# Choosing experts for the last eight attention pairs one step later, and reordering the scatters around it

## What is computed

```python
x = x + _L0_xattn_ref(_layernorm(x), ctx, ctx, mask, Wq, bq, Wk, bk, Wv, bv, Wo, bo)
# FFN on xt = x of the line above, per token:
router_logits = xt @ Wr + br
gates = max(softmax(router_logits)); idx = argmax(router_logits)
xn = layernorm(xt) * ln_g + ln_b
h = relu(xn @ W1[idx] + b1[idx]);  y = (h @ W2[idx] + b2[idx]) * gates
out = xt + y
```

## Time and profile before

| what | value |
|---|---|
| median of 3 runs (lowest to highest) | 268.44 us (268.17 to 268.88) |
| the profiled execution's own time, and its span | 265.34 us, 263.5 us |
| busy: PE, DVE, ACT, POOL | 243.8, 218.1, 171.7, 141.7 us |
| indirect DMA issues on POOL to DRAM (line 430) | 32, mean 1017 ns |
| last softmax shift begins (line 836) | 157.05 us |
| first expert matmul (line 1208) | 180.45 us |
| last expert matmul ends | about 254.5 us |

### The profile page before, as it was taken

The page is one execution under the profiler, slowest core; times in us unless marked ns, Lnnn a source line. Parts: engine busy times, 40 slices in busy tenths (PEclk is TensorE's granted clock), DMA queues, the critical chain, the costliest instruction groups (busy, mean ns, idle before and its releaser), DMA issues.

```text
span 263.5 us, 9102 instructions
## 1 busy us (share of the span) xinstructions
PE 243.8 (93%) x3204; PEld 191.2 (73%) x3204; DVE 218.1 (83%) x690; ACT 171.7 (65%) x339; POOL 141.7 (54%) x170
## 2 busy tenths in 40 slices
PE   8799999999999999999996999897999999999960
PEld 3266676785876777776854768446999999999950
DVE  7776878998999989987989897765889999999950
ACT  2697886876875967868754345004588888888820
POOL 3764363356658667765766546740454545454550
PEclk9999999999999999999999999999999999999996
DMA  7779980000000000000000100034122131222100
GB/s 190 236 226 348 412 348 6 2 2 7 20 13 13 13 24 21 16 10 23 13 23 21 36 23 23 31 115 107 50 55 72 50 87 57 74 72 65 42 23 0
DMA packets 17483, 19.55 MB, mean 74 GB/s; under 512 B 2703, under 2 KB 13332, under 8 KB 17440
## 3 DMA queue, kind: packets, MB, share of 16 engines
q1 hardware_dynamic: 14016, 14.15, 17.0%
q0 software_dynamic: 2272, 4.27, 4.7%
q10 hardware_dynamic: 1152, 0.57, 0.9%
HBM read 14.11 MB, written 5.33 MB: 74 GB/s over the span
## 4 chain that ended last, share of the span: by engine, by line
PE 69%; DVE 17%; issue 5%; POOL 3%; DMA 2%; POOLq 1%; ACT 1%; DVEq 0%; SPq 0%; ACTq 0%
PE ps L1208 13%; PE ps L1219 13%; PE ps L1026 8%; PE ps L1039 8%; PE ps L1132 7%; DVE Pr L836 5%; DVE mx L829 4%; PE ps L1065 4%; PE ps L1128 4%; PE ps L1011 3%; PE ps L1096 3%; PE ps L1201 2%; PE ps L1066 1%; PE ps L1103 1%; PE ps L1052 1%
## 5 line engine op out<-in xcount | busy, mean ns | idle before, releaser
L526 POOL DMA_INDIRECT out<-ot,G x39 | 37.8, 970 | 44.4 <-DVE ot L995 44.1
L551 ACT ACTIVATE PT<-ps 128x512 f32<-128x512 f32 x64 | 34.7, 594 | 31.8 <-PE ps L1039 31.6
L829 DVE TENSOR_REDUCE mx<-ps 128x16 f32<-128x1024 f32 x32 | 39.2, 1224 | 11.7 <-PE ps L1132 11.1
L430 POOL DMA_INDIRECT rows_dram<-row,posi x32 | 32.5, 1017 | 17.2 <-issue 9.6
L469 POOL TENSOR_TENSOR Kb<-KT,hmask 128x512 f32<-128x512 f32 x32 | 33.2, 1039 | 15.8 <-PE ps L1132 13.7
L1026 PEld LDWEIGHTS ps<-VB,PT 128*64 128x64 f32 x1024 | 32.4, 138 | 12.1 <-issue 12.1
L598 ACT ACTIVATE Pr<-Pr,rowany 128x1024 f32<-128x1024 f32 x32 | 36.8, 1149 | 4.3 <-DVE Pr L836 4.2
L836 DVE TENSOR_TENSOR Pr<-ps,mx 128x1024 f32<-128x1024 f32 x32 | 38.9, 1214 | 0.2
L1026 PE MATMUL ps<-VB,PT 128*64 128x18 f32 x1024 | 35.5, 212 | 0.0
L1039 PE MATMUL ps<-ident,Pr 128*128 128x128 f32 x256 | 34.7, 278 | 0.0
L1208 PE MATMUL ps<-xg,WR 128*128 128x128 f32 x248 | 32.8, 275 | 0.0
(11 more groups left out here) (133 smaller groups left out, 420.0 us busy)
## 6 DMA issues: line engine op xcount, KB each, us to landing
WA<-in_wpk SPq DMA_DIRECT2D x8, 578.0 KB, 11.0
G<-rows_dram SPq DMA_DIRECT2D x39, 66.0 KB, 1.9
X<-in_x SPq DMA_DIRECT2D x8, 256.0 KB, 6.1
C<-in_ctxT SPq DMA_DIRECT2D x8, 256.0 KB, 6.3
XT<-in_xT SPq DMA_DIRECT2D x8, 256.0 KB, 6.7
out<-ot,G POOLq DMA_INDIRECT x39, 2.2
rows_dram<-row,posi POOLq DMA_INDIRECT x32, 2.3
rows_dram<-empty ACTq DMA_DIRECT2D x6, 66.0 KB, 1.9
```

What stands on the lines that cost most here:

```text
L430: g.indirect_dma_start(out=rows, out_offset=bass.IndirectOffsetOnAxis(ap=posi[:, r, k:k + 1], axis=0), in_=row[:, r, k, E:E + RW], in_offs ...
L526: g.indirect_dma_start(out=out, out_offset=bass.IndirectOffsetOnAxis(ap=G[:, q, D + 1:D + 2].bitcast(I32), axis=0), in_=ot[:, q, :], in_of ...
L551: a.activation(PT[:, p % 2, 512 * m:512 * m + 512], ps[:, 4 + m, :], ACT.Copy).then_inc(freed[4 + m], 1)
L829: v.tensor_reduce(out=mx[:, i % 2, :], in_=psS.rearrange("p g (i k) -> p g i k", k=S), axis=AX.X, op=ALU.max).then_inc(s_mx, 1)
```

## The change

Five edits belong together:

- Unit 5 is scaled, picked and turned into one-hot rows in step 28 and ranked in step 29 (before: 27 and 28). Its ranks now share bank 7 with unit 6's second projection; its row numbers, gate and totals follow in step 30.
- Unit 6 is picked and made one-hot in step 31, after the softmax shift of pair 31 (before: step 30, ahead of pair 31's maxima). Its rank is computed behind unit 7's projection, and read behind the loop.
- Unit 6's first residual and its statistics come ahead of the reading of unit 5's ranks in step 29.
- GpSimd: the scatters of units 4 and 5 come later in the queue (behind `base_rows(8)`, behind the scores of pair 29, behind the power of unit 6), the power of unit 7 behind one scatter of unit 6 rather than two; all four scatters of unit 5 stand ahead of `scored(31)`.
- The three copies of the bias into `xb`, all in step 4 before, are made one a step in steps 5, 6 and 7.

```diff
     if u == NU - 4:
-        at.update(pick=last + 5, ranks=last + 6)
+        at.update(scale=last + 6, pick=last + 6, ranks=last + 7)
     if u == NU - 3:
-        at.update(o1=last + 3, scale=last + 4, pick=last + 4, ranks=last + 5)
+        at.update(o1=last + 3, scale=last + 4, pick=last + 5, ranks=last + 5)
...
-BANK = {("r", NU - 4): 7, ("o1", NU - 3): 7, ("onT", NU - 2): 7, ("r", NU - 3): 7, ("onT", NU - 1): 7,
+BANK = {("o1", NU - 3): 7, ("onT", NU - 2): 7, ("r", NU - 3): 7, ("onT", NU - 1): 7,
...
         def shares(u):
-            return u < NU - 4
+            return u < NU - 3
...
-                if (u := unit_at(i - 1, "scale")) is not None:
+                u = NU - 4 if i == NP - 4 else unit_at(i - 1, "scale")
+                if u is not None:
...
-                if i >= NP - 5:
-                    send(NU - 5, [i - NP + 5])
+                if i == NP - 5:
+                    send(NU - 5, [0])
...
             head_blocks(NP - 1)
-            send(NU - 5, [2])
             base_rows(NU - 1)
+            send(NU - 5, [1])
             scored(NP - 3)
-            send(NU - 5, [3])
-            send(NU - 4, [0, 1, 2])
+            send(NU - 5, [2, 3])
             rstd2(NU - 3)
             token_ids(NU - 3)
-            send(NU - 4, [3])
+            send(NU - 4, [0, 1, 2, 3])
             scored(NP - 1)
-            send(NU - 3, [0, 1])
+            send(NU - 3, [0])
             rstd2(NU - 2)
             token_ids(NU - 2)
-            send(NU - 3, [2, 3])
+            send(NU - 3, [1, 2, 3])
...
-                wait(dve, s_bo, 3 if u == m == 0 else 0)
+                wait(dve, s_bo, u + 1 if u < 3 and m == 0 else 0)
...
-                    for q in range(3):
-                        v.tensor_copy(xb[:, q, :, 0:E], bo_e[:, None, 0:E].to_broadcast([P, GP, E])).then_inc(s_bo, 1)
-                if (u := unit_at(i, "ranks")) == NU - 4:
-                    one_hot(u)
-                if (u := unit_at(i, "ranks")) is not None:
+                if 5 <= i < 8:
+                    v.tensor_copy(xb[:, i - 5, :, 0:E], bo_e[:, None, 0:E].to_broadcast([P, GP, E])).then_inc(s_bo, 1)
+                if i == NP - 3:
+                    residual(NU - 3, 0)
+                    stats2(NU - 3, 0)
+                if (u := unit_at(i, "ranks")) is not None and u != NU - 3:
                     read_ranks(u)
+                if i == NP - 2:
+                    places(NU - 4)
+                    gate(NU - 4)
+                    seen(NU - 4)
                 if i == NP - 1:
-                    places(NU - 3)
-                    gate(NU - 3)
+                    pick(NU - 3)
+                    one_hot(NU - 3)
                     normalise(i - 2)
...
+            read_ranks(NU - 3)
+            places(NU - 3)
+            gate(NU - 3)
+            seen(NU - 3)
             normalise(NP - 2)
             normalise(NP - 1)
             scale_logits(NU - 2)
...
-                if unit_at(i, "ranks") == NU - 3:
-                    rank(NU - 3)
                 if 0 <= i - 1 < NP:
                     transpose_p(i - 1)
...
                     project_o(u, 0)
+                if unit_at(i, "ranks") == NU - 3:
+                    rank(NU - 3)
                 if (u := unit_at(i, "o1")) is not None:
                     project_o(u, 1)
...
-                if (u := unit_at(i, "ranks")) == NU - 4:
-                    rank(u)
```

More of the change, by code:

```diff
@@ L112, in fill_order @@
             bank[6].append(("weights", i - 2))
-        for name, u in (("r", unit_at(i, "ranks") if i >= NP - 4 else None), ("o0", unit_at(i, "o0")), ("o1", unit_at(i, "o1")), ("onT", unit_at(i, "onT"))):
+        for name, u in (("r", unit_at(i, "ranks") if i == NP - 1 else None), ("o0", unit_at(i, "o0")), ("o1", unit_at(i, "o1")), ("onT", unit_at(i, "onT"))):
             if u is not None and (name != "o1" or len(part(u, 1))):
@@ L849, in _ @@
                     dve.wait_ge(freed[6], nth("weights", 2))
-                    for q in range(3):
-                        v.tensor_copy(xb[:, q, :, 0:E], bo_e[:, None, 0:E].to_broadcast([P, GP, E])).then_inc(s_bo, 1)
-                if (u := unit_at(i, "ranks")) == NU - 4:
-                    one_hot(u)
-                if (u := unit_at(i, "ranks")) is not None:
+                if 5 <= i < 8:
[4 more added lines that the diff above has]
+                if (u := unit_at(i, "ranks")) is not None and u != NU - 3:
                     read_ranks(u)
+                if i == NP - 2:
+                    places(NU - 4)
+                    gate(NU - 4)
+                    seen(NU - 4)
                 if i == NP - 1:
-                    places(NU - 3)
-                    gate(NU - 3)
+                    pick(NU - 3)
+                    one_hot(NU - 3)
                     normalise(i - 2)
-                if (u := unit_at(i, "o0")) is not None:
+                if (u := unit_at(i, "o0")) is not None and i != NP - 3:
                     residual(u, 0)
@@ L866, in _ @@
                     clear_v(2)
-                if (u := unit_at(i, "ranks")) is not None and u < NU - 3:
+                if (u := unit_at(i, "ranks")) is not None and u < NU - 4:
                     places(u)
-                if (u := unit_at(i - 1, "pick")) is not None and u < NU - 3:
+                if (u := unit_at(i - 1, "pick")) is not None and u < NU - 4:
                     gate(u)
@@ L872, in _ @@
                     scale_logits(u)
-                if (u := unit_at(i, "pick")) is not None and u < NU - 2:
+                if (u := unit_at(i, "pick")) is not None and u < NU - 3:
                     pick(u)
-                if (u := unit_at(i - 1, "pick")) is not None and u < NU - 2:
+                if (u := unit_at(i - 1, "pick")) is not None and u < NU - 4:
                     seen(u)
-                if (u := unit_at(i, "o0")) is not None:
+                if (u := unit_at(i, "o0")) is not None and i != NP - 3:
                     stats2(u, 0)
@@ L884, in _ @@
                     stats1(p)
-                if (u := unit_at(i, "pick")) is not None and u < NU - 2 and u != NU - 4:
+                if (u := unit_at(i, "pick")) is not None and u < NU - 3:
                     one_hot(u)
```

## The result

The changed kernel took 273.57 us (median of 6 runs, 272.70 to 275.85) against 268.13 us for the kernel before (6 runs, 266.53 to 268.88): slower by 2.0% by these medians, where 266.4 us was forecast. The ratio on record is 1.0258, 95% interval 1.0217 to 1.0299; it comes out as the mean of the six, 273.99 us, over the mean of the last three runs of the kernel before, 267.09 us (266.65, 268.10 and 266.53). The profiled execution took 273.64 us, its span is 271.8 us.

What follows compares the result with a forecast made beforehand. Bounds: the chain of waits, mostly TensorE, leaving it at VectorE's long instructions in step 27 and GpSimd's scatters behind the last shift. Bias 0.5 plus tail 1.5 gives 2.0 us: 268.44 to 266.4 us, bounds 266.0 to 267.4.

Steps and rivals of the forecast that it cites:

- The steps up to pair 31's maxima: Bias copies and steps 27 to 31: pair 5's maxima 0.5 us earlier, pair 30's 2.8, pair 31's 2.9.
- rival C: Scatters hold up VectorE's choosing by up to 1.0 us; the tail gains nothing, giving 267.9 us; 13 in 100.
- the strict reading of the Trainium skill's rule: Any GpSimd operation reading SBUF, scatters included, stops a VectorE operation with two SBUF inputs; it would give 267.9 us.
- scatters alone do not: Key blocks stop a VectorE operation with two operands in SBUF; a scatter running without them does not.
- The steps behind the last shift: VectorE and GpSimd after pair 31's softmax shift: unit 6's gate 0.35 us earlier, unit 8's power 1.5 us earlier.
- Behind the last shift, GpSimd: GpSimd's queue after pair 31's shift: unit 5's scatters out of the way by 157.8, unit 8's power 1.5 us earlier.
- the sum: 0.5 us from the bias copies and 1.5 us from the tail: 2.0 us in all.
- rival D: TensorE's clock falls to 1.2 GHz ahead of `rank(8)` and stays into the experts: 270.4 us; 5 in 100.
- the wait ahead of `rank(8)`: A new TensorE wait of 0.9 us, as 18 idle matmuls end before VectorE's one-hot rows come.

Runs made afterwards that it cites:

- e5: The changed kernel run again with no edit, on a prompt chip: 263.98 us, ratio 0.9898.
- e2: The changed kernel with three more idle matmuls, one ahead of pair 29's transposes and two ahead of pair 30's, on a prompt chip: 264.00 us, ratio 0.9871.
- e4: The changed kernel with 30 already satisfied waits added to TensorE's queue at about 7 us, on a prompt chip: 263.98 us, ratio 0.9918.
- e14: The changed kernel with unit 5's four scatters moved to the end of GpSimd's order, on a late chip: 270.05 us, ratio 1.0117.
- e9: The changed kernel run a third time with no edit, on a late chip: 272.86 us, ratio 1.0225.
- e18: The changed kernel with twelve idle matmuls on TensorE ahead of pair 31's transposes, on a late chip: 266.58 us, ratio 0.9995.
- e13: The kernel before, run again with no edit, on a late chip: 267.04 us, ratio 0.9993.
- e11: The kernel before with eight idle matmuls in TensorE's wait of step 28, on a late chip: 267.06 us, ratio 1.0011.
- e6: The kernel before with 30 already satisfied waits on TensorE behind its first projection of keys, on a prompt chip: 268.95 us, ratio 1.0064.
- e7: The kernel before with one idle matmul more in step 29 and two more in step 30, on a prompt chip: 270.26 us, ratio 1.0140.
- e17: The changed kernel with five idle matmuls on TensorE ahead of pair 31's transposes, on a prompt chip: 263.98 us, ratio 0.9919.
- e16: The changed kernel with twelve idle matmuls on TensorE ahead of pair 31's transposes, on a prompt chip: 265.68 us, ratio 0.9933.
- e1: The kernel before with only the three bias copies spread over steps 5 to 7, on a prompt chip: 268.29 us, ratio 1.0063.
- e10: The changed kernel with five further copies on ScalarE ahead of pair 30's real ones, on a late chip: 276.88 us, ratio 1.0364.

## Why the prediction was wrong, by its own steps

**The steps up to pair 31's maxima were right.** Pair 5 at 33.10 (33.1), pairs 28, 30 and 31 at 138.19, 148.44 and 152.54 (138.1, 148.3, 152.4). No choosing operation beside a scatter was over 0.19 us. That excludes rival C for these operations, and the strict reading of the Trainium skill's rule for them with it ("SBUF — State Buffer", SBUF: two separate sides): taken to cover scatters it would have made `pick(6)` up to 1 us longer, and its last instruction and `one_hot`, beside the scatter of 155.26, took 0.18 and 0.19 us (155.38 and 155.60). It doesn't settle the long `lsub` of the kernel before: that began at 139.04, 0.75 us ahead of the key blocks (139.79), and was not done when they began. Beside it ran a scatter:

```profile
138.69 1.08 POOL L430 DMA_INDIRECT rows_dram<-row,posi  x1 [0.18 <-PE ps L1132]
```

So the prediction's "scatters alone do not" doesn't fit it, and what held it for these 0.75 us stays open.

**The steps behind the last shift were right on a prompt chip.** In e5 unit 6's first scatter came at 159.05 (159.0), unit 8's power at 165.00 (165.0) right behind a scatter, the last transfer at 172.43 (172.2, so 1.7 us earlier than before where 2.0 was forecast), and `scale_logits(7)` waited 1.23 us for GpSimd. Profiled executions of e2 and e4 with the clock at 1.00 took 262.94 and 263.26 us; 263.3 was forecast for the changed kernel.

**The step that failed** is the sentence of *Behind the last shift, GpSimd*: "Unit 5's four scatters start at 153.0 and end by 157.8, so they are out of the way." They started at 152.64 and ended at 157.50, and on a late chip they were not out of the way. They lie beside `attend(29)`, the transposes of pair 30 and unit 7's projection, whose completions the last round of the attention waits for. In the profile of the kernel before, a row of four scatters lay from 146.68 to 151.5 and a single one at 153.77, so the last two rounds of the attention ran beside one scatter and not a row of four:

```profile
146.68 0.99 POOL L430 DMA_INDIRECT rows_dram<-row,posi  x1 [3.63 <-issue]
...
150.52 0.97 POOL L430 DMA_INDIRECT rows_dram<-row,posi  x1 [0.30 <-issue]
```

e14 shows the cause by taking the row away from there: no late completion between 153 and 157, and no fall of the clock before 169.36. The prediction put the cost of the row beside the last rounds at nothing; on late chips it measured 8.9 to 9.6 us with the clock it cost. And the sum had no term for the clock, which rival D put at 5 in 100.

**Rival D was the right kind and the wrong place.** It named the wait ahead of `rank(8)`; the clock fell behind another one, 2.76 us at 156.4. Its price, 4 us of TensorE's work at half clock, was too low: the half clock lasted 17.07 us in the first profile and 13.65 in e9's.

**How the loss divides.** On late chips the changed kernel took 273.57 and 272.86 us, with the clock kept (e18) 266.58, on prompt ones 263.98. So the lateness itself costs 2.6 us (266.58 less 263.98) and the halved clock 6.3 to 7.0 (272.86 and 273.57 less 266.58), 8.9 to 9.6 in all. Each of these comes from another chip, and the kernel before alone has medians from 266.33 to 267.60 us on the three late ones, so they are good to about 1 us. Two profiled executions of the changed kernel point the same way: with 13.65 us at half clock it took 272.13 us (e9), with 17.07 us 273.64, 1.5 us more for 3.4 us more. Set against the kernel before, one thing more counts on a late chip: it doesn't have 1.7 us of the stall there (e13, e11).

**On prompt chips the gain was about the forecast's 2.0 us or more**: 1.8 us between the lowest executions (264.82 to 263.06), 2.7 by the ratio (0.9898, its interval 1.3 to 4.1 us), 4.1 in the medians (268.12 to 263.98). I read what goes beyond 2.0 as the clock. The kernel before has executions of 268 to 271 us at 0.97 to 0.98, and e6 and e7, which differ from it little, lose it right behind the wait of step 28; the changed kernel's profile has no such wait (6.68 of 7.00 us busy). That the wait is the reason is argued and not shown: the first profile of the kernel before has the same wait (1.88 us, TensorE busy 1.34 of the 3.80 us from 141.00) and kept its clock, and e11, which filled it, ran on a late chip and told nothing.

**What stays open.** What in a row of scatters holds up TensorE's completions, why some beside it and not others, and why on some chips (or at some times) only, no run shows. The ends of matmuls in a profile are modelled, so the runs don't tell either whether the products themselves were late or only the word of them. Of the six chips of the experiments three were late. The first three runs of the kernel before were made at another time than those of the changed kernel; their profile shows no late completion and has the long `lsub`, as the prompt chips' have, while the changed kernel was profiled on a late one. So the 268.44 us that the forecast started from and the 273.57 us may belong to two kinds of chip; on one late chip the changed kernel took 6.5 us more than the kernel before (272.86 and 266.33).

The version that lost on neither kind is the changed kernel with twelve idle matmuls: 0.7% under the kernel before on a prompt chip (ratio 0.9933, 2.6 us by the medians), level with it on a late one (0.9995). Each was measured on one chip.

## What to carry to other kernels

When a row of GpSimd scatters is moved, ask which TensorE results are waited for beside it, not only which engines it occupies: a row that ends in time for GpSimd can still lie on the critical round. Where a wait of TensorE like those here (1.9 and 2.8 us) can open, idle matmuls in front of it are cheap (e17: no cost, e16: 1.7 us) beside what the clock took (6 to 7 us). And a forecast of 1% should be measured on more than one chip before its mechanism is judged; here the same code took more, less and again more than the kernel before (ratios 1.0258, 0.9898, 1.0225).

## What the runs showed of the hardware

- One program ran in two ways, each chip in one of them (chip and moment not told apart). On late ones some of TensorE's completions beside GpSimd's scatters arrived late, at the same places in every profile of the changed kernel: up to 1.0 us beside two scatters (143 to 145), up to 4.2 us beside four (153 to 157). Others beside such a row did not (e14 at 161.89 and 162.35, e13 at 148.67). On prompt ones none was over 0.35 us late.
- For a wait on such a completion the profile names no releaser ("remote", "another core or an unknown queue"), though only one core runs. Between 20 and 178 us no profile from a prompt chip has that label. It can be missing: e14, with at most 0.7 us, and e13, with at most 1.8, have none.
- The same instruction beside the same scatter and key block, `lsub` at 139.04, took 1.88 us on the chip of the profile before and 1.86 on prompt chips (e1, e6, e7), and 0.19 us on the late chips of e11 and e13.
- Once fallen, the granted clock was at half for 3.4 us (e13, from 144.80) up to 20.5 us (e10, from 159.08); 17.07 us in the first profile of the changed kernel, from 159.17. Falls of 3.4 us came at the start of the experts as well (e5 from 178.95, e14 from 183.01, e18 from 182.87).
